# The experts' up product of a gated mixture layer as seven half products for eight, with weight and row sums on GpSimd and rows scattered from the accumulator

## What is computed

```python
    buf = jnp.zeros((E * C + 1, D), x.dtype).at[slot].set(xf[tokens])
    xb = buf[:E * C].reshape(E, C, D)
    gu = jnp.einsum('ecd,efd->ecf', xb, w12)
    g, u = jnp.split(gu, 2, axis=-1)
    h = jax.nn.silu(g) * u
    yb = jnp.einsum('ecf,edf->ecd', h, w3).reshape(E * C, D)
    ys = yb[jnp.minimum(slot, E * C - 1)] * (weights * kept.astype(weights.dtype))[:, None]
    out = jnp.zeros((T, D), x.dtype).at[tokens].add(ys)
```

## Time and profile before

| | us |
|---|---|
| three executions | 2812.26, 2815.03, 2813.39 |
| their median | 2813.39 |
| the profiled execution: span from the first to the last instruction | 2811.9 |
| TensorE busy with matmuls | 2682.0 (95%) |
| VectorE busy | 1397.9 (50%) |
| ScalarE busy | 983.7 (35%) |
| GpSimd busy | 415.5 (15%) |
| stage of the experts, from the first turned row to the end | 606.4 to 2811.9 |

### The profile page before, as it was taken

One profiled execution on the slowest core, in us unless ns is written; L12 is line 12 of the kernel. 1 busy time (PEld: TensorE's weight loads), 2 busy tenths in 40 slices (PEclk: granted clock), 3 DMA queues, 4 the chain that ended last, 5 costly groups with the idle time before them and its releaser, 6 DMA issues.

```text
span 2811.9 us, 41356 instructions
## 1 busy us (share of the span) xinstructions
PE 2682.0 (95%) x14486; PEld 2409.9 (86%) x14487; DVE 1397.9 (50%) x2725; ACT 983.7 (35%) x2543; POOL 415.5 (15%) x393
## 2 busy tenths in 40 slices
PE   6999999839999999999999999999999999999987
PEld 5888888839999888888888788888888899989976
DVE  5777777624444444444444444454444444444555
ACT  4766666412222322233222332232222322233343
POOL 3454554410000100011000200010000100030030
PEclk9999999959999999999999999999999999999999
DMA  7522222132101401123101321121111411033142
GB/s 257 199 82 75 84 90 73 63 136 83 34 33 52 109 27 41 45 60 83 45 22 45 78 88 45 67 57 75 45 45 29 112 45 45 34 72 122 67 122 78
DMA packets 60031, 208.33 MB, mean 74 GB/s; under 512 B 9564, under 2 KB 9836, under 8 KB 51602
## 3 DMA queue, kind: packets, MB, share of 16 engines
q1 hardware_dynamic: 43282, 175.30, 17.3%
q0 software_dynamic: 16640, 31.69, 5.9%
HBM read 145.60 MB, written 67.70 MB: 76 GB/s over the span
## 4 chain that ended last, share of the span: by engine, by line
PE 74%; issue 2%; DVE 1%; ACT 1%; DMA 0%; DVEq 0%; POOL 0%; ACTq 0%; POOLq 0%
PE bank L1396 74%; PE bank L1402 1%; DVE yacc L1335 1%; DVE slotsT_lo L1303 0%; ACT slotsT_hi L1217 0%; DMA raw<-in_moe_w_dram 0%; DVE h L1355 0%; DVE w_lo L1290 0%; ACT w_hi L1213 0%; POOL out_dram L1193 0%; DVE w_lo L1297 0%; ACT h_hi L1258 0%; ACT yout L1244 0%; DVEq L1334 0%; DVEq L1301 0%
## 5 line engine op out<-in xcount | busy, mean ns | idle before, releaser
L1396 PE MATMUL bank<-slotsT_hi,w_hi 128*128 128x384 f32 (+2 forms) x2560 | 888.0, 347 | 25.3 <-issue 22.1
L1396 PE MATMUL bank<-slotsT_lo,w_hi 128*128 128x384 f32 (+2 forms) x2560 | 885.4, 346 | 0.0
L1396 PE MATMUL bank<-slotsT_hi,w_lo 128*128 128x384 f32 (+2 forms) x2560 | 883.9, 345 | 0.0
L1355 DVE TENSOR_TENSOR h<-silu,bank 128x384 f32<-128x384 f32 (+2 forms) x320 | 183.8, 575 | 831.6 <-PE bank L1396 830.6
L1396 PEld LDWEIGHTS bank<-slotsT_hi,w_hi 128*128 128x128 f32 x2560 | 483.5, 189 | 57.3 <-issue 25.7
L1396 PEld LDWEIGHTS bank<-slotsT_lo,w_hi 128*128 128x128 f32 x2560 | 483.8, 189 | 24.9
L1396 PEld LDWEIGHTS bank<-slotsT_hi,w_lo 128*128 128x128 f32 x2560 | 483.5, 189 | 21.6
L1258 ACT CAST h_hi<-h 128x384 fp32r<-128x384 f32 (+2 forms) x320 | 169.3, 529 | 745.4 <-DVE h L1355 745.4
L1252 ACT ACTIVATE silu<-bank 128x384 f32<-128x384 f32 (+2 forms) x320 | 162.5, 508 | 727.5 <-PE bank L1396 727.0
L1335 DVE TENSOR_TENSOR yacc<-bank,yacc 128x512 f32<-128x512 f32 x464 | 317.9, 689 | 183.8 <-PE bank L1396 176.3
L1396 PE MATMUL bank<-w_hi,h_hi 128*128 128x512 f32 x1008 | 401.3, 398 | 7.1 <-DVE yacc L1335 7.1
(11 more groups left out here) (158 smaller groups left out, 2921.7 us busy)
## 6 DMA issues: line engine op xcount, KB each, us to landing
raw<-in_moe_w_dram SPq DMA_DIRECT2D x65, 1536.0 KB, 6.2
xrow<-expert_rows SPq DMA_DIRECT2D x42, 520.0 KB, 9.1
expert_rows<-zeros SPq DMA_DIRECT2D x40, 520.0 KB, 8.1
xin<-in_x_dram SPq DMA_DIRECT2D x16, 512.0 KB, 3.7
xres<-in_x_dram SPq DMA_DIRECT2D x16, 512.0 KB, 3.7
out_dram<-xres SPq DMA_DIRECT2D x16, 512.0 KB, 3.5
probs<-in_L_xattn_Wq_dram SPq DMA_DIRECT2D x1, 1024.0 KB, 11.3
probs<-in_L_xattn_Wo_dram SPq DMA_DIRECT2D x1, 1024.0 KB, 6.5
```

What stands on the lines that cost most here:

```text
L1355: nc.vector.tensor_tensor(h32[q % 2][:, 0:W], silu[q % 2][:, 0:W], UB[q % 2][:, 0:W], ALU.mult)\
L1396: last = nc.tensor.matmul(out_ap, st, mv, start=(at == 0), stop=(at == n - 1))
```

## The change

The up product of a tile of hidden units is a product of 2 x 2 parts: the weights are cut into gate and up rows and into two halves of the width 512, the slots into two halves of 64 in each tile and the same two halves of the width. One level of Strassen's scheme (Winograd's form) makes the four results from seven **half products** in place of eight. A half product is 2 tiles of the width x 3 passes = 6 matmuls, with 64 columns for each tile of slots.

- **Weights.** For each `j` GpSimd makes four sums of 256 columns from the raw weights (`sums`, `last_sum`): S1 to S4. ScalarE and VectorE split 7 x 256 columns in three units (`u0`, `u1`, `u2`: 512, 768, 512 columns) and `w3` (512) in place of 1024 + 512. The raw weights come in four smaller DMAs a chunk, single buffered.
- **Rows.** ScalarE copies the four parts of a turned tile from the bank to `xsum` (`x_copy`), GpSimd makes four sums of 128 columns (`x_sums`), ScalarE the high and VectorE the low parts of seven parts (14 x 64 columns). `xsum` has two buffers. Seven tiles (`XA`) are turned at the end of the expert before, whatever number of tiles the next one has, and tiles 7 to 9 in chunk 0.
- **A step** is one `j` and one block. Blocks are now 3 to 7 tiles (192 to 448 columns); 8, 9 and 10 tiles are cut in two (4+4, 5+4, 5+5). A step's products are P1 and P2, then those of the step before that are late (P4, P3), then P6, S3T3 and P5. Down products stand in slots a, b and c between them. The accumulating banks are read on the way: ScalarE copies P1 (`kept_p1`), P1+P6 (`kept_u2`) and P1+P6+P5 (`kept_u4`), VectorE adds P2 (`c11_ready`), S3T3 (`c22_ready`) and S3T3+P4 (`c21_ready`).
- **Output.** VectorE multiplies a down product by the row's weight while it adds it to `yacc`, so the last `yacc` is scattered as it is. GpSimd scatters all ten tiles, tiles 0 to 4 at the end of an expert, 5 to 9 in chunk 0 of the next one, then waits for them to land and clears `yacc` (`slot_weights`). Nothing of `yout` and `nothing` is left.

```diff
-BLOCKS = {3: (3,), 4: (2, 2), 5: (3, 2), 6: (3, 3), 7: (4, 3), 8: (4, 4), 9: (3, 3, 3), 10: (4, 3, 3)}
+MID = {3: (3,), 4: (4,), 5: (5,), 6: (6,), 7: (7,), 8: (4, 4), 9: (5, 4), 10: (5, 5)}
+LAST = {**MID, 6: (3, 3), 7: (4, 3)}
-XA = 4
+XA = 7
...
+A11, A12, S1, S2, S3, S4, A22 = range(7)
+T1, T2, T3, T4, B21, B22, B11, B12 = range(8)
...
+        def sums(j, loads, g):
+            a11, a21, a12, a22 = quarters(j)
+            pool.wait_ge(up_loaded[j], loads)
+            if not isinstance(g, int) or g > 0:
+                pool.wait_ge(u1_lo, g)
+            nc.gpsimd.tensor_tensor(wsum[:, 0, :], a21, a22, ALU.add).then_inc(s1_ready, 1)
+            nc.gpsimd.tensor_tensor(wsum[:, 2, :], a11, a21, ALU.subtract).then_inc(sums_made, 1)
+            pool.wait_ge(s1_ready, g + 1)
+            nc.gpsimd.tensor_tensor(wsum[:, 1, :], wsum[:, 0, :], a11, ALU.subtract).then_inc(sums_made, 1)
+        def last_sum(j, g):
+            a11, a21, a12, a22 = quarters(j)
+            pool.wait_ge(u0_lo, g + 1)
+            pool.wait_ge(sums_made, g * 2 + 2)
+            nc.gpsimd.tensor_tensor(a12, a12, wsum[:, 1, :], ALU.subtract).then_inc(s4_ready, 1)
+        def x_sums(i, at, copied, t1, t2, done):
+            v = xsum[i % 2]
+            pool.wait_ge(copied, at)
+            nc.gpsimd.tensor_tensor(v[:, T1, :], v[:, B12, :], v[:, B11, :], ALU.subtract).then_inc(t1, 1)
+            nc.gpsimd.tensor_tensor(v[:, T3, :], v[:, B22, :], v[:, B12, :], ALU.subtract)
+            pool.wait_ge(t1, at)
+            nc.gpsimd.tensor_tensor(v[:, T2, :], v[:, B22, :], v[:, T1, :], ALU.subtract).then_inc(t2, 1)
+            pool.wait_ge(t2, at)
+            nc.gpsimd.tensor_tensor(v[:, T4, :], v[:, B21, :], v[:, T2, :], ALU.subtract).then_inc(done, 1)
...
-                for t in reversed(range(NT)):
-                        in_=yout[:, i, :] if t < nt else nothing[:, :], in_offset=None,
+            for tiles in (slice(0, SA), slice(SA, NT)):
+                nc.gpsimd.memset(yacc[:, tiles, :], 0.0).then_inc(y_cleared, 1)
+        def scatter(t, at, done):
+            wait_apart(pool, "pool", y_added, at)
+            nc.gpsimd.indirect_dma_start(
+                out=out_tok, out_offset=bass.IndirectOffsetOnAxis(ap=token[:, t:t + 1], axis=0),
+                in_=yacc[:, t, :], in_offset=None,
+                bounds_check=T - 1, oob_is_err=False, compute_op=ALU.add).then_inc(done, 16)
...
+            if kind == "first":
+                left = list(range(SA, NT))
+                for i in rest_at(nt, 0) + rest_at(nt, 1):
+                    x_sums(i, XB * e + i - XA + 1, xb_cp, xb_t1, xb_t2, xb_t)
+                    if i > XA:
+                        scatter(left.pop(0), tiles_before(e, 0) + 1, added_b)
...
+                sums(0, loads, g + 2)
+                if n_steps(nt, kind) == 2:
+                    last_sum(0, g + 2)
+                for t in left:
+                    scatter(t, tiles_before(e, 0) + 1, added_b)
+                slot_weights(e)
+                if n_steps(nt, kind) > 2:
+                    last_sum(0, g + 2)
+                sums(1, loads, g + 3)
+                last_sum(1, g + 3)
...
+                    next_sums(e, 2, 3, 4)
+                    for t in range(2):
+                        scatter(t, added_at(t), added_a)
+                    next_sums(e, 5, 6)
+                for t in range(2, SA):
+                    scatter(t, added_at(t), added_a)
+        experts(pool, chunk)
+        for t in range(SA, NT):
+            scatter(t, tiles_before(E, 0) + 1, added_b)
...
+                nc.scalar.copy(gu[par][:, 0, 0:W], X[par][:, 0:W]).then_inc(kept_p1, step_of(nt, kind, s))
+                act.wait_ge(c11_ready, base + 1 + upto(nt, kind, s))
+                nc.scalar.activation(gu[par][:, 0, 0:W], gu[par][:, 0, 0:W], ACT.Silu)\
+                  .then_inc(silu1_ready, step_of(nt, kind, s))
+                units(s, "early")
+                if before_it:
+                    second_silu(*before_it)
...
+                gate_first = before_it and downs_at(nt, kind, s, "b")
+                if gate_first:
+                    h_high(*before_it)
+                act.wait_ge(p6_done, base + upto(nt, kind, s))
+                nc.scalar.copy(ug[par][:, 0, 0:W], X[par][:, 0:W]).then_inc(kept_u2, step_of(nt, kind, s))
+                if before_it and not gate_first:
+                    h_high(*before_it)
...
+                nc.scalar.copy(gu[par][:, 1, 0:W], X[par][:, 0:W]).then_inc(kept_u4, step_of(nt, kind, s))
+                units(s)
+                if kind == "first" and s == 0:
+                    for i in rest_at(nt, 0):
+                        rest_high(i)
...
+                nc.vector.scalar_tensor_tensor(out=yacc[:, t, :], in0=YB[t % 2][:, :], scalar=wslot[:, t:t + 1],
+                                               in1=yacc[:, t, :], op0=ALU.mult, op1=ALU.add)\
+                  .then_inc(y_added, tile_of(nt, t))
...
-                    passes(GB[q % 2][:, 0:W], list(zip(stat(j), moving))).then_inc(g_ready, step_of(nt, q))
-                    passes(UB[q % 2][:, 0:W], list(zip(stat(NJ + j), moving))).then_inc(u_ready, step_of(nt, q))
+            def product(out, of, j, b, a_of, b_of, opens, closes):
+                W, cols, n = width(nt, of, b), half_cols(nt, of, b), 0
+                for k in range(2):
+                    st_hi, st_lo = w12_hi[j][:, 2 * a_of + k, :], w12_lo[j][:, 2 * a_of + k, :]
+                    mv_hi, mv_lo = xT_hi[:, 2 * b_of + k, cols], xT_lo[:, 2 * b_of + k, cols]
+                    for st, mv in ((st_hi, mv_hi), (st_hi, mv_lo), (st_lo, mv_hi)):
+                        ins = nc.tensor.matmul(out[:, 0:W], st, mv, start=opens and n == 0,
+                                               stop=closes and n == 5, skip_group_check=True)
...
+                pe.wait_ge(c22_ready, at)
+                pe.wait_ge(u2_lo, g_of + j + 1)
+                product(Y, of, j, b, A22, T4, False, True).then_inc(p4_done, step_of(nt, of, s))
+                product(X[s % 2], of, j, b, S4, B22, False, True).then_inc(p3_done, step_of(nt, of, s))
...
+                pe.wait_ge(silu2_ready, base + 1 + back(nt, kind, s, 2))
+                product(X[par], kind, j, b, A11, B11, True, False).then_inc(p1_done, step_of(nt, kind, s))
+                pe.wait_ge(c11_ready, base + 1 + back(nt, kind, s, 1))
+                product(Z, kind, j, b, A12, B21, True, True).then_inc(p2_done, step_of(nt, kind, s))
+                downs(s, "a")
...
+                if before_it:
+                    late_products(*before_it, g if s > 0 else g - NJ)
+                downs(s, "b")
+                pe.wait_ge(kept_p1, base + upto(nt, kind, s))
...
+                product(X[par], kind, j, b, S2, T2, False, False).then_inc(p6_done, step_of(nt, kind, s))
+                pe.wait_ge(c21_ready, base + 1 + back(nt, kind, s, 1))
+                product(Y, kind, j, b, S3, T3, True, False)
+                pe.wait_ge(kept_u2, base + upto(nt, kind, s))
+                product(X[par], kind, j, b, S1, T1, False, False).then_inc(p5_done, step_of(nt, kind, s))
+                downs(s, "c")
...
```

899 lines of the change are left out of this document (573 added, 326 removed).

## The result

The kernel after takes 2917.6 us (median of 4 runs, 2915.1 to 2924.6) against 2813.6 for the kernel before on the same chip: ratio 1.0377, interval 1.0363 to 1.0391. So it is slower, as forecast, but by 104 us and not by 9, and it lies outside the range of 2765 to 2885. The profiled execution has a span of 2922.8 us, 110.9 above that of before. Of the four it is the slowest, 7 us above their median, so what is read from its trace is some 7 us too large.

What follows compares the result with a forecast made beforehand. TensorE, busy 95% of the span, was taken to bound the kernel. Terms of -148 + 4 + 20 + 98 + 10 + 20 + 5 = +9 us on the median of 2813.4 gave 2822 us, range 2765 to 2885 (8 in 10).

Steps and rivals of the forecast that it cites:

- Term 1: Up product on TensorE: half products save 148 us over all experts; eight more turned tiles add 4.
- third rival: Up product: half products don't gain, 192 to 320 columns being paced by weight loads; well over 2900 us, chance 0.02.
- Term 2: Waits inside middle chunks: none with ten and seven tiles, 0.3, 0.8, 1.5 us a chunk with nine, five, three; +20 us.
- Term 3: Each expert's start: waits for GpSimd's queue of sums, scatters, landing and clearing of yacc; together +98 us.
- Term 4: The two ends: later first start, +10 us; useless tiles' sums and eight scatters after the last addition, +20 us.
- Term 5: VectorE and GpSimd at one memory port: +5 us, bounds 0 and 95.
- second rival: Narrow experts: VectorE's two-operand SBUF reads and GpSimd's sums delay each other; 2891 us, half of it 2854; chance 0.15.

Runs made afterwards that it cites:

- later_downs: Kernel after, with the first down product moved from behind P5 of step 0 to behind P2 of step 1 in one-block middle chunks; 2911.3 us.
- scatters_behind: Kernel after, with GpSimd's scatters queued behind the sums of rows at both places of a change of expert; 2946.9 us.
- clear_early: Kernel after, with yacc tiles 0 to 4 cleared while the scatters of tiles 5 to 9 land, not behind them; 2903.6 us.
- before_gap: Kernel before, with eight ScalarE copies of 512 columns at each expert's chunk 0 and TensorE made to wait for them; 2897.5 us, ratio 1.0294.

## Why the prediction was wrong

- **Term 1, -148: right.** Measured -139. The pitches are 0.1468 and 0.201 as taken; at 192 columns 0.1113, so of the two bounds the transposes' 0.107 was the nearer, not the line's 0.090. The third rival (no gain from narrow products) is out.
- **Term 2, +20: failed.** Chunks 2 to 6 alone, five of the eight in each expert, lose 54.7 us (some 48 where the three- and five-tile chunks keep to 16.9 and 22.1). The step that failed: "Ten and seven tiles come out without a wait". Seven lose 1.9 us a chunk, five 2.8 for 0.8, three 3.4 for 1.5. I followed P6, P5 and the late products, but not the last link: late P3, silu, gate, high part, low part, and the first down product that asks for it after 18 products. later_downs shows that this link is late: it takes 1.2 us off a seven-tile chunk and 0.9 off a five-tile one. The early units of weights ahead of the second silu, which the prediction names for three tiles, hold it up with five tiles too.
- **Term 3, +98: failed in size, at the right places.** Less 55 in middle chunks and 17 at the end, 174 of the 246 us lie in the first expert's start and the chunks 0, 1 and 7 (45 of them in chunks 1), where terms 3 and 5 and the start of term 4 had 98 + 5 + 10 = 113. This is the larger part of what was missed. ScalarE did wait for GpSimd (`xsum` 42.5 us, `raw_up` 25.1, `wsum` 30.6), and of the chain that I followed, scatter, landing and clearing proved the one that decides (scatters_behind +29, clear_early -14). What the sum left out is the price of turning seven tiles where no GpSimd is involved: I had +4 for the transposes and charged the rest only through GpSimd's chain; by itself, in the kernel before, it costs +20.
- **Term 4: +20 about right, +10 not separated.** The last addition ends at 2893.3, the span 29.5 later, against 12.7 before: +17. The prologue and first expert together gave +16 where I had 0 by the sum of its parts (-23 + 11 + 2 + 10).
- **Term 5, +5: too small.** About 24 of bounds 0 to 95. The second rival, GpSimd and VectorE in each other's way, had the mechanism right and its place wrong: it names the narrow middle chunks, which don't change without the sums of weights; the cost lies at the change of expert, where both have a full queue. The rule that I cited for this term agrees with these traces; its price was a quarter of the upper bound.
- **No term at all for the clock: 39 us.** The earlier trace rows showed 1.00 in wide experts and 0.94 in the last, and the sum added waits as if each cost its length. before_gap shows that a wait costs 1.2 to 1.9 us beyond its length; the 39 us are a count in the trace of after, and no run took them away by themselves.

By place, of the 93 us missing 35 lie in the middle chunks and 61 at the changes of expert, and the tail has 3 less than forecast. By cause they are the clock (39), the port (19 more than forecast), the seven tiles (16 more) and the late `h_lo`, which overlap and don't add up to a checked sum. The excess at the starts was not separated further into GpSimd's queue, waits put down to "issue" (32.0 us in 7 waits; in the kernel before 22.1 in 8) and VectorE's full queue. The direction came out as forecast, but at +9 us, with a chance of 0.33 for faster, the sum had hardly decided it; 93 us of waiting did.

## What to carry to other kernels

Count the waits, not only their length: a change that cuts one engine's work into shorter pieces between more handshakes can pay for a fall of the matrix engine's clock at each of them. Follow every hand-over to its last consumer, and at a change of phase write down all queues side by side, since postponing one item of a full queue (scatters here) may cost more than it frees. A saving of 139 us in the steady state was worth less than 8 changes of expert (174 us more waiting).

## What the runs showed of the hardware

- A stretch of products at about twice their distance, with windows granted 0.50, cost 1.6 us on average, in most cases 1.0 to 2.5. In before_gap it cost 1.2 to 1.9 us, about the same behind a wait of 3 us and of 16 us.
- A chunk of the same instructions ran at 22.1 or at 23.6 us for several chunks in a row, at a mean granted clock of 1.00 or 0.93; its longest wait is 1.5 us in both. What decides between them stays open.
- GpSimd's and VectorE's two-operand instructions from SBUF lengthened each other, mostly by up to the other's length (VectorE 0.69 to 1.23 us, GpSimd 0.73 to 1.57), once by three sums in a row (VectorE 1.09 to 3.58). The clearing of `yacc` (2.23 to 2.26 us), additions with one operand in a bank (0.74 to 0.75 for 512 columns) and ScalarE's `h_hi` (0.72 to 0.73 for 640 columns) kept their lengths in the kernel after.
- At the start of the three-tile expert ScalarE stood idle for 6.4 us, put down to "issue", between the last instruction of the old body and a table load of the new one. TensorE waited 9.6 us for the copy behind it:

```profile
2722.66 0.94 ACT L1445 CAST slotsT_hi<-xsum 128x896 fp32r<-128x896 f32 x1 [1.57 <-POOL xsum L1294]
2729.99 1.28 ACT L1507 ACT_TABLE_LOAD   x1 [6.40 <-issue]
```
